# A graph-network kernel on one core: the segment sums of a chunk run one step later, beside the other native float32 products, and the backward masks are read from the forward ones

## The reference, cut to what matters

```python
def tensor_product(x_e, sh, w, C):              # C: [64, 9, 128]
    acc = sh[:, 0:1] * (x_e @ C[:, 0, :])
    for s in range(1, 9):
        acc = acc + sh[:, s:s + 1] * (x_e @ C[:, s, :])
    return acc * w

# layer 0: edge_index = [src, dst]; each edge reads x[src], and is summed at its dst
wk = relu(edge_attr_64 @ k_w1 + k_b1) @ k_w2 + k_b2        # wv alike
k = tensor_product(x[src], edge_attr_9, wk, Cqk)           # 8 heads of 16; v alike, with wv, Cv
attn = einsum('ehd,ehd->eh', (x @ Wq)[dst], k)
ex = exp(attn - segment_max(attn, dst)[dst])
upd = segment_sum(v * ex, dst) / segment_sum(ex, dst)
x1 = layernorm(x + batchnorm(x @ W_self + upd @ W_out))
# layer 1
agg = segment_sum(edge_attr_64, dst) / max(counts, 1)
y = relu(relu(concat(agg, x1) @ W0 + b0) @ W1 + b1) @ W2 + b2
out = layernorm(x1 + y)
```

## Time and profile before

| | |
|---|---|
| runs | 5020.54, 5025.04, 5040.35 us; median 5025.04 us |
| profiled execution, its own time | 5049.76 us |
| its span, first to last instruction | 5047.8 us |
| mean granted TensorE clock | 0.975 |
| busy: PE, DVE, POOL, ACT | 95%, 80%, 74%, 68% of the span |
| DMA | mean busy share of the 16 engines 88% over queues q0 and q1; 199 GB/s over the span |

### The profile page before, as it was taken

The page is one execution under the profiler, slowest core; times in us unless marked ns, Lnnn a source line. Parts: engine busy times, 40 slices in busy tenths (PEclk is TensorE's granted clock), DMA queues, the critical chain, the costliest instruction groups (busy, mean ns, idle before and its releaser), DMA issues. The chain is left out here.

```text
span 5047.8 us, 115383 instructions
## 1 busy us (share of the span) xinstructions
PE 4772.7 (95%) x35582; PEld 4503.5 (89%) x35582; DVE 4058.6 (80%) x5044; ACT 3414.7 (68%) x6495; POOL 3713.3 (74%) x3494
## 2 busy tenths in 40 slices
PE   7999999999999999999999999999999999998256
PEld 6999999999999999999999999999999999998143
DVE  5888888888888888888888888888888888886435
ACT  2677677677777767767777677777777777776137
POOL 3777777777777777777777777777777777774460
PEclk9999999999999999999999999999999999998578
DMA  8899999999999999999999999999999999996220
GB/s 218 202 215 210 208 210 214 208 214 210 212 207 214 213 208 213 211 210 211 211 213 211 207 216 213 216 214 214 213 216 212 214 214 216 212 213 158 91 68 26
DMA packets 693458, 1006.45 MB, mean 199 GB/s; under 512 B 120054, under 2 KB 378168, under 8 KB 693160
## 3 DMA queue, kind: packets, MB, share of 16 engines
q1 hardware_dynamic: 574856, 753.93, 65.7%
q0 software_dynamic: 112960, 242.16, 22.7%
q10 hardware_dynamic: 5600, 9.83, 0.7%
HBM read 826.64 MB, written 178.93 MB: 199 GB/s over the span
## 5 line engine op out<-in xcount | busy, mean ns | idle before, releaser
L825 PE MATMUL psum<-chi,zhi 128*128 128x256 f32 x7840 | 2316.9, 301 | 2.2 <-DVE rv L731 2.1
L535 POOL DMA_INDIRECT gq<-qtab,idxs x1568 | 1881.1, 1200 | 478.0 <-issue 475.8
L828 PE MATMUL psum<-clo,zhi 128*128 128x256 f32 x7840 | 2144.4, 282 | 0.0
L530 POOL DMA_INDIRECT gx<-in_xg,idxs x1568 | 1555.4, 992 | 465.0 <-issue 453.5
L827 PE MATMUL psum<-chi,zlo 128*128 128x256 f32 x6272 | 1768.4, 282 | 0.0
L825 PEld LDWEIGHTS psum<-chi,zhi 128*128 128x128 f32 x7840 | 1478.6, 189 | 99.3 <-issue 99.3
L828 PEld LDWEIGHTS psum<-clo,zhi 128*128 128x128 f32 x7840 | 1476.2, 188 | 0.0
L827 PEld LDWEIGHTS psum<-chi,zlo 128*128 128x128 f32 x6272 | 1183.6, 189 | 93.0 <-issue 93.0
L685 DVE TENSOR_TENSOR z<-psum,shb 128x1536 f32<-128x1536 f32 (+1 forms) x784 | 1130.5, 1483 | 126.2 <-PE psum L797 118.7
L580 ACT ACTIVATE zhi<-z 128x1536 fp32r<-128x1536 f32 (+1 forms) x784 | 993.5, 1267 | 247.9 <-DVE z L685 244.0
L710 DVE TENSOR_TENSOR zlo<-z,zhi 128x1536 fp32r<-128x1536 f32 (+1 forms) x784 | 922.2, 1217 | 0.0
(11 more groups left out here) (210 smaller groups left out, 6335.1 us busy)
## 6 DMA issues: line engine op xcount, KB each, us to landing
shb<-in_shT SPq DMA_DIRECT2D x392, 640.0 KB
shb<-in_shT SPq DMA_DIRECT2D x392, 512.0 KB
rows<-ot SPq DMA_DIRECT2D x392, 416.0 KB
e<-in_eT SPq DMA_DIRECT2D x392, 128.0 KB
drow<-rankd SPq DMA_DIRECT2D x392, 128.0 KB
gx<-in_xg,idxs POOLq DMA_INDIRECT x1568
gq<-qtab,idxs POOLq DMA_INDIRECT x1568
qtab<-qs ACTq DMA_DIRECT2D x25, 256.0 KB, 5.7
```

The lines of the kernel that those rows point to most:

```text
L530: nc.gpsimd.indirect_dma_start(out=gx[:, s, k, :], out_offset=None, in_=xg[:, :], in_offset=bass.IndirectOffsetOnAxis(ap=ids[:, k:k + 1], ...
L535: nc.gpsimd.indirect_dma_start(out=gq[:, s, k, :], out_offset=None, in_=qtab[:, :], in_offset=bass.IndirectOffsetOnAxis(ap=ids[:, TC + k:T ...
L825: mm(tpb[:, k, :], zhi[:, s, j, e], chi[:, j, :], start=(j == 0), stop=False)
L828: last = mm(tpb[:, k, :], zhi[:, s, j, e], clo[:, j, :], start=False, stop=(j == ST - 1))
```

## The change

1. One step later. PE, ACT and SP get a third chunk, a = t-7. PE's order in step t becomes sums(a, 0), turned_x(c), hidden(c), sums(a, 1), tensor_products(t), [turned_features], edge_weights(c). SP stores chunk t-8 in place of t-7. The loop ends one step later.
2. ACT's order in step t becomes sums(a, 0), edge_weights(t), weights(b), hidden(c), sums(a, 1), maxima(a), z_first_part(c, 0), hidden_first_part(c), z_first_part(c, 1), [feature_rows], segments(b). `LAG` and the numbers of buffers of `ot`, `drow` and `seg` (two each) stay, and so does SP's `targets(t-4)` with its wait.
3. `nmb` is dropped: the backward scan reads `nmf` shifted by one column, with a constant mark in column 128. One 32 KB transfer of two goes from each fourth step, with a small store and a memset in the preparation.
4. The constant tiles of the edge loop are freed after it (addresses only), and the last block's 17 counters become three, one for each engine that counts, with the same conditions.

```diff
-    for n in range(R0 + UN * TURNS, NC + LAG + 2):
+    for n in range(R0 + UN * TURNS, NC + LAG + 3):
...
@@ SyncE
-                        for ahead, tile in ((0, nmf), (1, nmb)):
-                            src = newd[bass.ds(g.value() * CH + ahead, GT * P)].rearrange("(t e) -> t e", t=GT)
-                            sp.dma_start(tile[:, s, :], src.unsqueeze(1).broadcast_to([GT, H, P])).then_inc(nm_in[s], 16)
+                        src = newd[bass.ds(g.value() * CH, GT * P)].rearrange("(t e) -> t e", t=GT)
+                        sp.dma_start(nmf[:, s, 0:P], src.unsqueeze(1).broadcast_to([GT, H, P])).then_inc(nm_in[s], 16)
...
-                        if (t + (-LAG - 1)).there():
-                            store(t + (-LAG - 1))
+                        if (t + (-LAG - 2)).there():
+                            store(t + (-LAG - 2))
@@ ScalarE
-                        c, b = t + 1, t + (-LAG)
+                        c, b, a = t + 1, t + (-LAG), t + (-LAG - 1)
+                        if a.there():
+                            sums(a, 0)
+                        if t.there():
+                            edge_weights(t)
                         if b.there():
                             weights(b)
-                        if t.there():
-                            edge_weights(t)
+                        if c.there():
+                            hidden(c)
+                        if a.there():
+                            sums(a, 1)
+                            maxima(a)
                         if c.there():
                             z_first_part(c, 0)
-                            hidden(c)
+                            hidden_first_part(c)
                             z_first_part(c, 1)
-                            hidden_first_part(c)
                             if c.r % 2 == 1:
                                 feature_rows(c + (-1))
                         if b.there():
-                            sums(b, 0)
-                            maxima(b)
-                        if (b + 1).there():
-                            segments(b + 1)
-                        if b.there():
-                            sums(b, 1)
+                            segments(b)
@@ VectorE
-                        v.tensor_tensor_scan(mr[:, ::-1], nmb[:, s, ::-1], mf[:, ::-1], -BIG, ALU.add, ALU.max).then_inc(mr_done, 1)
+                        v.tensor_tensor_scan(mr[:, ::-1], nmf[:, s, P:0:-1], mf[:, ::-1], -BIG, ALU.add, ALU.max).then_inc(mr_done, 1)
@@ TensorE
-                        c, b = t + 1, t + (-LAG)
+                        c, a = t + 1, t + (-LAG - 1)
+                        if a.there():
+                            sums(a, 0)
                         if c.there():
                             turned_x(c)
                             hidden(c)
+                        if a.there():
+                            sums(a, 1)
                         if t.there():
                             tensor_products(t)
                         if c.there() and c.r % 2 == 1:
                             turned_features(c + (-1))
-                        if b.there():
-                            sums(b, 0)
                         if c.there():
                             edge_weights(c)
-                        if b.there():
-                            sums(b, 1)
```

More of the change, by code:

```diff
@@ L104, in gnn_kernel @@
     qtab = dram("qtab", (NP, O), fp32)
-    newd = dram("newd", (EP + P,), bf16)
+    newd = dram("newd", (EP,), bf16)
     chaind = dram("chaind", (EC,), fp32)
@@ L116, in sem @@
             return ctx.enter_context(nc.semaphore(name))
[L119 to L126, removed]
         wout = sb("wout", [O, 2, P])
@@ L151, in gnn_kernel, with eb @@
         banks = [psum[:, i * 512:(i + 1) * 512] for i in range(8)]
+        edges = ctx.enter_context(ExitStack())
+        def eb(name, shape, dt=fp32):
+            return edges.enter_context(nc.sbuf_tensor(name, shape, dt))
+        chi = eb("chi", [P, ST, KV], f32r)
+        clo = eb("clo", [P, ST, KV], f32r)
+        w1 = eb("w1", [P, 2, P])
+        b1c = eb("b1c", [P, 1])
+        w2hi = eb("w2hi", [P, KV], f32r)
+        w2lo = eb("w2lo", [P, KV], f32r)
+        b2hl = eb("b2hl", [P, KV], f32r)
+        ones = eb("ones", [P, P], f32r)
+        idx_all = eb("idx_all", [P, 2 * EC], i32)
+        ndcol = eb("ndcol", [P, EC])
         load = sem("load")
@@ L220, in _ @@
                         sp.dma_start(dst, src).then_inc(load, 16)
-                    sp.wait_ge(neg_made, 3)
-                    sp.dma_start(newd[0:EP].rearrange("(p c) -> p c", p=P), neg[:, :]).then_inc(tables_stored, 16)
-                    sp.dma_start(newd[EP:EP + P].rearrange("(p c) -> p c", p=2), npad[:, :]).then_inc(tables_stored, 16)
+                    sp.wait_ge(neg_made, 2)
+                    sp.dma_start(newd.rearrange("(p c) -> p c", p=P), neg[:, :]).then_inc(tables_stored, 16)
                     sp.wait_ge(rank_made, 6)
@@ L229, in _ @@
                     sp.wait_ge(load, 16 * len(consts))
-                    sp.wait_ge(tables_stored, 64)
+                    sp.wait_ge(tables_stored, 48)
                 @block.tensor
@@ L378, in gnn_kernel @@
             drow = ms("drow", [P, 2, CH], bf16)
-            nmf = ms("nmf", [P, 2, P], bf16)
-            nmb = ms("nmb", [P, 2, P], bf16)
+            nmf = ms("nmf", [P, 2, P + 1], bf16)
             hid = ms("hid", [P, CH])
@@ L744, in segment_maxima @@
                         dve.wait_ge(at_full, n)
-                        dve.wait_ge(nm_in[s], 32 * (g.turn(2 * GC) + 1))
+                        dve.wait_ge(nm_in[s], 16 * (g.turn(2 * GC) + 1))
                         if g.old(GC):
                             dve.wait_ge(mt_full, n - 1)
-                        v.tensor_tensor_scan(mf[:, :], nmf[:, s, :], sbank[:, 0:P], -BIG, ALU.add, ALU.max).then_inc(mf_done, 1)
+                        v.tensor_tensor_scan(mf[:, :], nmf[:, s, 0:P], sbank[:, 0:P], -BIG, ALU.add, ALU.max).then_inc(mf_done, 1)
                         dve.wait_ge(mf_done, n)
-                        v.tensor_tensor_scan(mr[:, ::-1], nmb[:, s, ::-1], mf[:, ::-1], -BIG, ALU.add, ALU.max).then_inc(mr_done, 1)
+                        v.tensor_tensor_scan(mr[:, ::-1], nmf[:, s, P:0:-1], mf[:, ::-1], -BIG, ALU.add, ALU.max).then_inc(mr_done, 1)
                     def below_maxima(g):
@@ L783, in _ @@
                     v.memset(shb[D:P, :, ST - 1, :], 0.0).then_inc(shb_zero, 1)
-                    dve.wait_ge(shb_zero, 1)
+                    v.memset(nmf[:, :, P:P + 1], -BIG).then_inc(shb_zero, 1)
+                    dve.wait_ge(shb_zero, 2)
                     steps(dve, step)
@@ L885, in _ @@
                     steps(pe, step)
+        edges.close()
         with ExitStack() as mend:
@@ L1085, in gnn_kernel @@
             st_d, st_a, st_pe = sem("stats_dve"), sem("stats_act"), sem("stats_pe")
[L1086 to L1089, removed]
+            MADE = {"pe": ("mean", "var", "z0", "z1", "z2", "mean2", "var2"),
+                    "act": ("r", "sq", "lg", "rs", "h0", "h1", "sq2", "lg2", "rs2"),
+                    "dve": ("y", "dd", "x1", "s0", "y2", "dd2", "o")}
+            made_by = {e: sem(f"blocks_made_by_{e}") for e in MADE}
             def wait_made(engine, name, i, j):
[L1093 to L1096, removed]
+                for e, names in MADE.items():
+                    if name in names:
+                        engine.wait_ge(made_by[e], (i * len(names) + names.index(name)) * GN + (j + 1))
             with ExitStack() as fin1:
@@ L1293, in product @@
                                 wait_made(pe, after, i, j)
-                                t.matmul(bank_of(j), lhsT[:, :], W(src, j), start=True, stop=True).then_inc(prod_made, 1)
+                                t.matmul(bank_of(j), lhsT[:, :], W(src, j), start=True, stop=True).then_inc(made_by["pe"], 1)
                         def turn(i):
@@ L1326, in each_block @@
                                 wait_made(act, after, i, j)
-                                fn(j).then_inc(SS[name], 1)
+                                fn(j).then_inc(made_by["act"], 1)
                         act.wait_ge(st_d, 6)
@@ L1333, in turn @@
                                 if past(i):
-                                    act.wait_ge(SS["o"], i * GN)
-                                f(W("r", j), xp[:, ncols(i, j)], ACT.Identity, bias=st[:, 9:10]).then_inc(SS["r"], 1)
+                                    wait_made(act, "o", i + (-1), GN - 1)
+                                f(W("r", j), xp[:, ncols(i, j)], ACT.Identity, bias=st[:, 9:10]).then_inc(made_by["act"], 1)
                             for j in range(GN):
@@ L1338, in turn @@
                                     act.wait_ge(y_s[j], i * 16)
-                                act.wait_ge(SS["dd"], i * GN + (j + 1))
-                                f(W("sq", j), W("dd", j), ACT.Square).then_inc(SS["sq"], 1)
+                                wait_made(act, "dd", i, j)
```

(3 more changed lines are left out.)

10 lines of the change are left out of this document (3 added, 7 removed).

## The result

The changed kernel takes 6218.73 us (median of 4 runs, 6202.29 to 6232.89), against 5022.79 us before: a ratio of 1.237, 95% interval 1.233 to 1.242. The profiled execution took 6232.89 us, its span is 6230.9.

The account below looks back on a forecast made before the run. PE was taken to bound the kernel before; the change adds a store cycle. First 7 steps 81 us plus 192 pairs of 29.0 + 0.5 make a 5745 us loop instead of 4542; with +20 at the end, 6250 us, range 5800 to 6850.

Parts of the forecast that it names:

- The store's place in SP's queue: SP's store stands behind targets waiting for seg, so each ACT step's first copy waits for it: 29.0 us a pair, not 23.2.
- copy to end of `seg`: On ACT, from the first copy of sums to the end of seg: 11.4 us for t even, 7.4 for t odd.
- landing: The store's transfer from SP's issue to its landing: 4.0 us, with 2.7 and 5.7 as ends.
- The pair: Two successive loop steps: 12.3 us for t odd, 16.6 for t even, 29.0 with wake-ups, plus 0.5 for PE's clock.
- A sign that did not come: Expected in the profile after: PE busy below 80% in the loop, waiting 3.9 and 1.3 us before sums(a, 1).
- PE's wait for `seg`: At the start of even steps PE needs the seg that ACT makes after feature_rows, and waits 1.05 us.
- rival 1: The store is in time and only PE's wait for seg on even steps bites: 5200 us, chance 0.08.
- The clock: After its wait PE runs at half clock for a while: 0.5 us a pair, with 0 and 2 as ends.
- rival 2: PE's clock stays low, at half in most even steps too: 8000 us, or 7100 for half of that; chance 0.11.
- Changes between product kinds: PE switching between native and split products costs 0, bounds 0 and 0.1 us per change; at most 40 us gained.
- Masks, addresses, counters: Fewer mask transfers already counted in the sum; addresses and counters of the last block: 0.
- Rival 3: PE saves its product changes (40 us) and gx waits (43.5) shrink, other waits hidden: 4940 to 4990 us, chance 0.05.

Follow-up runs that it names:

- experiment 1: Changed kernel with SP issuing the store of chunk t-8 ahead of targets and masks: 5381.99 us, ratio 1.072 to the kernel before.
- experiment 2: Changed kernel with SP's step beginning with the store, ahead of harmonics, features, targets and masks: 5197.36 us, ratio 1.030 to the kernel before.
- experiment 4: Changed kernel with both repairs, the store ahead of the targets and ACT's segments(b) ahead of feature_rows: 4957.54 us, ratio 0.987 to the kernel before.
- experiment 8: Changed kernel with 30 unused transposes on PE in each step with t odd, between hidden and the second half of sums: 6081.73 us.
- experiment 6: Kernel with the store ahead of the targets and seg early, but with the addresses of the kernel before: 4976.63 us, ratio 0.987.
- experiment 5: Kernel before with only masks, addresses and counters changed: 5073.83 us; only constant tiles moved: 5064.56; only the tiles behind the masks moved: 5077.44.

## Why the prediction was right

Forecast 6250 us, measured 6218.73.

- **The store's place in SP's queue.** Right, and shown: experiments 1 and 2 move only that store and take away 1021 of the 1196 us; `seg` early on top (experiment 4) takes the rest. By terms: copy to end of `seg` 11.4 and 7.4 forecast, 11.4 and 7.7 measured (medians); SP 0.9 forecast, 0.98 measured; SP with a mask transfer 1.5 forecast, 1.9 measured; landing 4.0 forecast, 3.8 on the profile's page. Two small terms stood in the sum without a row: 0.05 for a wake-up, which is 0.09 from the store's landing to the copy, and 0.15 from the copy to the sums, which is 0.05 after a wait. No run separates a fixed cost of the store from the time of its bytes. The pair was to be 29.5 and is 29.4.
- **Part of that nearness is luck.** With the clock held up (experiment 8) the pair is 28.6 us, where the sum had 29.0 without the clock's share. That share was 0.5 and is 0.7 to 0.8, so the two misses nearly cancel.
- **A sign that did not come.** PE was to be busy below 80% in the loop and is at 85% (683.85 of 800 us). Its wait before the second half of sums is 3.2 us on steps with t odd (median), where 3.9 was forecast, and nothing on the others, where 1.3 was.
- **PE's wait for `seg`**, 1.05 us on even steps. Right. In the changed kernel it is inside the store cycle; rival 1 had it alone at 5200 us, and experiment 2, which is that rival's case, gave 5197. That is nearer than the reasoning: against experiment 6, which differs from it in the place of the store and of `seg` and in the constants' addresses, the even steps are 1.2 us longer in the mean and not 1.05, but the shorter spacing takes 0.2 off the pair. A point missed there: a store that is merely issued in time isn't landed in time when it stands behind 1.4 MB of other transfers on the same queue (experiment 1).
- **The clock.** The term was too small: 0.5 us a pair, 96 us, forecast; the fill gave 137 us. Its reasoning was right: in about half of the pairs PE is late in the odd step by more than its slack, and there PE's sums and not the store end ACT's wait. The clock fell and came back, as in rows 10, and was at half for 758 us of the loop in all, so rival 2 (it stays low) didn't happen. The Trainium skill's account of a clock that is lost in each tile ("TensorE: Matmul & The Clock Gate", "HAM oscillation") describes what is seen, 178 falls in the loop for 192 pairs of steps, but each cost 0.7 us of 29 and not half of the work.
- **Changes between product kinds cost nothing.** Right, measured at under 0.005 us each, against a bound of 0.1.
- **Masks, addresses, counters: 0.** Wrong in size. With the orders of before they cost 1.1%, with longer waits for `gx`; the shift of the tiles behind the masks alone does the same (experiment 5). In the changed kernel PE isn't the bound and this couldn't show.
- **Rival 3 (faster)** asked for a store some 4 us earlier. With the two repairs it exists: 4957.54 us, inside its 4940 to 4990. Of its two reasons one held, the waits for `gx` shrink, and the other did not, since changes of kind cost nothing; the shorter spacing stands in its place.

What the repaired version gains from can be read from the traces. The order itself leaves PE's own step as it was: a pair of steps without a wait is 22.83 us in experiment 6 and 22.84 with the masks moved and the old order (experiment 5). Against the 23.07 us of the kernel before, the shorter spacing gives some 46 us, and the constants' addresses give 18 more (experiment 6). The rest is the waits for `gx`, of which only those at the start of the loop are left, 20.6 us in place of 43.5 (rows 4) or of 85.6 with everything but the reordering:

```profile
PE psum L802 <- DMA gx<-in_xg,idxs: 20.6, 3, 15.8
```

So the gathers keep up with the same PE step at which they fell behind in the old order. By the profile's rough spans of GpSimd, a step's eight gathers keep it busy 8.2 to 8.5 us in the repaired versions, and 8.8 to 8.9 in the kernel before and the runs of experiment 5. That the new order puts VectorE's and GpSimd's work in a better phase would explain this; no run here separated it.

## What to carry to other kernels

When a step is moved later in a software pipeline, follow every wait of the in-order queues that stand between it and its consumer, the transfer queue first: a store that shares a queue with a load inherits that load's wait. Count the round trip (compute, issue, landing, compute) against the length of a step; two buffers cover it only if the issue isn't tied to the end of the same step. If such a cycle appears, put the store ahead of whatever waits and, if it is still waited for, ahead of the large loads, and make early what the queue of transfers waits for, before judging the reordering itself: here the store's place and `seg` made early turned 24% slower into 1.3% faster.

## What the runs showed of the hardware that was not expected

- The spacing of split products of 256 columns was 0.120 or 0.118 us, by where the loop's tiles behind the masks lay: a shift of some 500 bytes a partition, 0.11 us a step. With the new order it fell to 0.113 us on every fourth step, by where the constants lay.
- A shorter spacing gave a slower kernel (ratio 1.010), as PE's waits for the gathers grew from 43.5 to 93.9 us and its clock was at half for 58 us in place of 10. It was not PE's pace alone: the repaired version keeps the same pace with 20.6 us of such waits.
- A 3.3 us wait of PE was followed by sums at half speed, 1.70 us for 0.84; and thirty useless transposes in that wait were worth 2.2% of the time.
